# Routing one-hots of a Mamba-plus-MoE block: place one-hots built without values on VectorE, top-2 taken from the logits, instruction order laid out anew

## The reference

```python
router_logits = x_flat @ gate_w                      # 2048 tokens x 8 experts
router_probs = jax.nn.softmax(router_logits, axis=-1)
topk_w, topk_idx = jax.lax.top_k(router_probs, TOP_K)          # TOP_K = 2
topk_w = topk_w / jnp.sum(topk_w, axis=-1, keepdims=True)
...
h = jax.nn.silu(ragged_dot(x_rep_sort, w1, group_sizes)) * ragged_dot(x_rep_sort, w3, group_sizes)
out_sort = ragged_dot(h, w2, group_sizes)            # M = 896
...
out = jnp.einsum('tkd,tk->td', out_rep, topk_w)
return x + out
```

## Time and profile before

| | us |
|---|---|
| median of 3 runs | 792.99 |
| range of the runs | 791.93 to 797.85 |
| the profiled execution, whole | 797.66 |
| its span, first to last instruction | 795.8 |
| PE busy in the span | 736.1 (93%) |
| DVE busy | 600.4 (75%) |
| POOL busy | 305.4 (38%) |
| ACT busy | 242.0 (30%) |
| mean granted PE clock | 0.954 |

### The profile page before, as it was taken

One profiled execution on the slowest core, in us unless ns is written; L12 is line 12 of the kernel. 1 busy time (PEld: TensorE's weight loads), 2 busy tenths in 40 slices (PEclk: granted clock), 3 DMA queues, 4 the chain that ended last, 5 costly groups with the idle time before them and its releaser, 6 DMA issues.

```text
span 795.8 us, 10296 instructions
## 1 busy us (share of the span) xinstructions
PE 736.1 (93%) x2771; PEld 476.5 (60%) x2772; DVE 600.4 (75%) x1486; ACT 242.0 (30%) x485; POOL 305.4 (38%) x506
## 2 busy tenths in 40 slices
PE   6979799999999999996679999999999999999993
PEld 4456565586558668664445666666666666666662
DVE  3899988698965676474436888888888888888880
ACT  1547737455784452311001111111111111111110
POOL 2142523333223622129962333444333444333322
PEclk9979989999999999996659999999999999999997
DMA  9402003000400360501008951121111112111111
GB/s 319 131 1 107 0 1 107 0 1 28 133 1 1 102 228 2 192 0 54 0 14 297 304 165 27 26 31 31 31 26 26 26 26 33 33 26 26 26 14 20
DMA packets 31437, 52.10 MB, mean 65 GB/s; under 512 B 3216, under 2 KB 23120, under 8 KB 31408
## 3 DMA queue, kind: packets, MB, share of 16 engines
q1 hardware_dynamic: 23920, 41.51, 15.1%
q0 software_dynamic: 7488, 10.23, 7.8%
HBM read 42.10 MB, written 9.63 MB: 65 GB/s over the span
## 4 chain that ended last, share of the span: by engine, by line
PE 70%; DVE 11%; POOL 8%; issue 7%; DMA 1%; ACT 1%; DVEq 0%; POOLq 0%
PE ps L1025 28%; PE ps L1038 14%; POOL big L2187 5%; PE ps L731 4%; PE ps L403 3%; PE ps L717 3%; PE ps L705 3%; PE ps L458 3%; DVE big L1544 3%; PE ps L582 2%; PE ps L525 2%; PE ps L472 2%; DVE big L1564 2%; DVE big L2070 2%; PE ps L539 1%
## 5 line engine op out<-in xcount | busy, mean ns | idle before, releaser
L2070 DVE STREAM_TRANSPOSE big<-big 32x224 f32<-32x224 f32 x608 | 244.8, 403 | 9.1
L1025 PE MATMUL ps<-big 128*128 x624 | 241.2, 539 | 1.1 <-ACT big L1450 1.1
L1025 PEld LDWEIGHTS ps<-big 128*128 128x128 f32 x624 | 118.4, 190 | 105.2 <-issue 103.4
L1038 PE MATMUL ps<-big 128*128 x546 | 124.5, 380 | 2.1 <-DVE big L2090 1.3
L2113 POOL TENSOR_TENSOR big<-big 128x1 f32<-128x1 f32 x153 | 48.2, 315 | 202.1 <-DVE big L2078 152.5
L1038 PEld LDWEIGHTS ps<-big 128*128 128x128 f32 x546 | 100.8, 190 | 15.0 <-issue 2.9
L1456 ACT ACTIVATE big<-ps 128x896 f32<-128x896 f32 x39 | 35.8, 917 | 215.6 <-PE ps L1025 215.6
L2085 DVE TENSOR_TENSOR big<-big,ps 128x896 f32<-128x896 f32 x39 | 42.4, 1088 | 48.3 <-PE ps L1025 48.2
L2336 POOL DMA_INDIRECT out_rows<-big x39 | 62.9, 1612 | 22.7 <-issue 22.7
L403 PEld LDWEIGHTS ps<-big 128*128 128x128 f32 x325 | 41.2, 145 | 46.6 <-issue 28.1
L403 PE MATMUL ps<-big 128*128 128x128 f32 x325 | 54.0, 281 | 14.0 <-DVE big L1645 3.5
(11 more groups left out here) (183 smaller groups left out, 967.5 us busy)
## 6 DMA issues: line engine op xcount, KB each, us to landing
big<-in_w SPq DMA_DIRECT2D x24, 896.0 KB, 7.6
big<-cum_rows SPq DMA_DIRECT2D x16, 512.0 KB, 5.3
out_rows<-big SPq DMA_DIRECT2D x4, 512.0 KB, 2.9
xn_rows<-big SPq DMA_DIRECT2D x4, 512.0 KB, 3.1
big<-in_hidden SPq DMA_DIRECT2D x1, 1536.0 KB, 12.1
big<-in_in_proj SPq DMA_DIRECT2D x1, 1288.0 KB, 7.1
big<-in_gate SPq DMA_DIRECT2D x1, 640.0 KB, 13.2
big<-in_up SPq DMA_DIRECT2D x1, 640.0 KB, 8.7
```

Source lines behind the costliest of these rows:

```text
L1025: last = mm(bank(bk + n)[:, 0:HALF], xT[:, k, :], expert_cols(e, off + k * M + n * HALF, HALF), start=(k == 0), stop=(k == KD - 1))
L1038: last = mm(bank(7)[:, 0:D], hTs[:, half, j * P:(j + 1) * P], expert_cols(e, 2 * KD * M + j * D, D), start=(j == 0), stop=(j == MB - 1))
L2070: last = V.transpose(hTs[c * SQ:(c + 1) * SQ, half, :].rearrange("p (j t) -> p j t", j=MB)[:, :, q * SQ:(q + 1) * SQ], ha[q * SQ:(q + 1) * ...
```

## The change

Per engine, what differs:

- **POOL**: the 64 `slots` instructions go.
- **DVE**: `slots(n)` is now one `is_equal` over 8 x 128 elements per sequence (4 x 128 per half), with no value in it. The values go to the list side: `route_block` multiplies token numbers and weights into the block one-hot, and `route_list(n, i)` writes one list for tokens and one for weights, 8 x 128 elements each (before: 4 x 128 each, one per choice). `route_hot` becomes `route_place` (3 instructions) and `route_block` (4).
- **Routing arithmetic on DVE**: top-2 is taken from the logits, with no softmax ahead; exp is taken of one difference per token and feeds only the weights (`route_weigh`, `route_rec`). `route_max` is gone; per part of the work 26 DVE instructions from the maximum to the slots where there were 33 (whole sequence).
- **PE**: `place_` makes for each chunk and choice two products of N = 128 instead of one of N = 256, after one product over zeros that opens the bank. `mlp_down(3, 3)` moves ahead of `turn_half(0)`. `WARM_ROWS` is 4.
- **Order**: the lists of all engines are written anew, in the first stage too; the last part of DVE's is below. `slots`, `route_place` and the lists of sequences 0 and 1 stand between the `hidden_(3, j)`, those of sequence 2 around the last `add_mlp`.

```diff
-WARM_START, WARM_LAST, WARM_ROWS = 5, 8, 5
+WARM_START, WARM_LAST, WARM_ROWS = 5, 8, 4
...
-                pe.wait_ge(hot_placed, nth(n, CH, t))
-                pe.wait_ge(hot_ready, TOP * (n + 1 if n < SEQS - 1 or t < CH // 2 else n + 2))
+                part = n if t < HALVES[0][1].stop or n < SEQS - 1 else SEQS
+                pe.wait_ge(hot_placed, part + 1)
+                pe.wait_ge(hot_ready, 2 * (part + 1))
                 if n == 0 and t == 0:
                     pe.wait_ge(off_scaled, SEQS * (CH - 1))
+
+                    mm(bank(STATES)[:, 0:2 * P], ident[0:P - REST, :], hid[0:P - REST, JB - 1, 0:2 * P], start=True, stop=False)
                 for k in range(TOP):
-                    last = mm(bank(STATES)[:, 0:2 * P], hot_list[n][:, t, k, :], hot_slot[n][:, t, k, :],
-                              start=(n + t + k == 0), stop=(n == SEQS - 1 and t == CH - 1 and k == TOP - 1))
+                    for i, hot in enumerate((hot_token, hot_weight)):
+                        last = mm(bank(STATES)[:, i * P:(i + 1) * P], hot[n][:, t * TOP + k, :], hot_slot[n][:, t * TOP + k, :],
+                                  start=False, stop=(n == SEQS - 1 and t == CH - 1 and k == TOP - 1 and i == 1))
...
             mlp_down(3, 0)
             mlp_down(3, 1)
             mlp_down(3, 2)
+            mlp_down(3, 3)
             turn_half(0)
-            mlp_down(3, 3)
             half_logits(0)
...
+            def route_pick(n, ts=ALL, seq=None):
+                seq = n if seq is None else seq
+                top_.start(n)
+                v.wait_ge(lg_taken, n + 1)
+                top_.then(V.tensor_reduce(rmx[:, ts], lg[:, ts, :], AX, ALU.max))
...
+            def route_next(n, ts=ALL, seq=None):
+                seq = n if seq is None else seq
+                o1, o2 = (picked[seq][:, ts, k, :] for k in range(TOP))
+                top_.then(V.scalar_tensor_tensor(rq[:, ts, :], o1, LEAST, lg[:, ts, :], ALU.mult, ALU.add))
+                top_.then(V.tensor_reduce(rmx2[:, ts], rq[:, ts, :], AX, ALU.max))
+                pick(rq, rmx2, o2, rm2, ts)
+                top_.end()
+                if 0 < n < SEQS:
+                    v.wait_ge(pos_ps, n)
+                V.tensor_tensor(sel[:, ts, :], o1, o2, ALU.add).then_inc(sel_ready, 1)
+
...
+            def route_weigh(n, ts=ALL):
+                v.wait_ge(sel_ready, n + 1)
+                if 0 < n < SEQS:
+                    v.wait_ge(route_e, n)
+                V.tensor_tensor(rd[:, ts], rmx2[:, ts], rmx[:, ts], ALU.subtract).then_inc(route_d, 1)
...
                 v.wait_ge(route_e, n + 1)
...
+                weigh_.start(n)
+                weigh_.then(V.tensor_scalar(rden[:, ts], re_[:, ts], 1.0, None, ALU.add))
+                weigh_.then(V.reciprocal(weight[seq][:, ts, 0], rden[:, ts]))
...
+                steps.then(V.tensor_tensor(picked_pos[:, ts, :, :], picked[seq][:, ts, :, :],
+                                           rpos[:, ts, :].unsqueeze(2).to_broadcast([P, ts.stop - ts.start, TOP, E]), ALU.mult))
+                steps.then(V.tensor_reduce(slotf[seq][:, ts, :], picked_pos[:, ts, :, :], AX, ALU.add))
...
+            def route_place(n, ts=ALL, seq=None):
...
                 v.wait_ge(ssy_ready, SEQS * CH)
                 hot_.start(n)
...
+                hot_.then(V.tensor_tensor(upto_q[:, q, :], entries(slotf[seq], ts).unsqueeze(2).to_broadcast([P, m, LIST + 1]), firsts, ALU.is_ge))
                 hot_.then(V.tensor_reduce(q1[:, q], upto_q[:, q, :], AX, ALU.add))
...
+            def route_block(n, ts=ALL, seq=None):
...
+                V.tensor_tensor(is_q[:, q, :], upto_q[:, q, 0:LIST], upto_q[:, q, 1:LIST + 1], ALU.subtract)
+                v.wait_ge(place_ready, n + 1)
+                hot_.then(V.tensor_tensor(token[:, ts, :], cst[:, at_ + ts.start:at_ + ts.stop].unsqueeze(2).to_broadcast([P, m // TOP, TOP]),
                                           place[seq][:, ts, :], ALU.subtract))
...
+                V.tensor_tensor(token_q[:, q, :], is_q[:, q, :], entries(token, ts).unsqueeze(2).to_broadcast([P, m, LIST]), ALU.mult)
...
+                hot_.then(V.tensor_tensor(weight_q[:, q, :], is_q[:, q, :], entries(weight[seq], ts).unsqueeze(2).to_broadcast([P, m, LIST]), ALU.mult))
...
+            def route_list(n, i, ts=ALL, seq=None):
                 seq = n if seq is None else seq
...
+                v.wait_ge(hot_step, 4 * (n + 1))
+                V.tensor_tensor((hot_token, hot_weight)[i][seq][:, q, :].rearrange("p k (e i) -> p k e i", e=E),
+                                picked[seq][:, ts, :, :].rearrange("p t k e -> p (t k) e").unsqueeze(3).to_broadcast([P, m, E, LIST]),
+                                (token_q, weight_q)[i][:, q, :].unsqueeze(2).to_broadcast([P, m, E, LIST]),
+                                ALU.mult).then_inc(hot_ready, 1)
...
+            def slots(n, ts=ALL, seq=None):
...
-                V.tensor_tensor(hot_list[seq][:, ts, k, :].rearrange("p t (e i) -> p t e i", e=E),
-                                picked[seq][k][:, ts, :].unsqueeze(3).to_broadcast([P, m, E, LIST]),
-                                is_q[seq][:, q, :].rearrange("p (t k) i -> p t k i", k=TOP)[:, :, k, :].unsqueeze(2).to_broadcast([P, m, E, LIST]),
-                                ALU.mult).then_inc(hot_ready, 1)
+                V.tensor_tensor(hot_slot[seq][:, q, :], cst[:, C_SLOT:C_SLOT + P].unsqueeze(1).to_broadcast([P, m, P]),
+                                entries(place[seq], ts).unsqueeze(2).to_broadcast([P, m, P]), ALU.is_equal).then_inc(hot_placed, 1)
...
             scores(0, 3)
             apart(1, 0, 0)
+            apart(1, 0, 1)
             state(0, 2)
-            apart(1, 0, 1)
-            h1_(0, 0)
 
             y_(0, 2)
+            masked_G(1)
+            apart(1, 1, 0)
+            ln1_h(2)
             off(0, 3)
-            masked_G(1)
-            ln1_h(2)
-            apart(1, 1, 0)
+            h1_(0, 1)
             apart(1, 1, 1)
-            scores(1, 0)
-            h1_(0, 1)
-            hT1(2)
 
...
+            route_weigh(1)
+            route_slots(1)
+            route_place(1)
+            slots(0)
+            hidden_(3, 0)
+            slots(1)
+            hidden_(3, 1)
+            route_list(0, 0, ALL, None)
+            route_list(0, 1, ALL, None)
             route_rec(1)
-            route_slots(1)
-            hidden_(3, 0)
-            hidden_(3, 1)
-            route_max(2, ALL, 0)
+            route_block(1)
...
             ln2_stats(3, HALVES[1][1], 4, 1)
-            route_max(3, HALVES[0][1], 3, half_rt)
             xn_(4, HALVES[1][1], 3)
-            route_hot(2)
-            route_pick(3, HALVES[0][1], 3, half_rt)
-            route_next(3, HALVES[0][1], 3, half_rt)
-            route_rec(3, HALVES[0][1], 3, half_rt)
             route_list(2, 0, ALL, None)
             route_list(2, 1, ALL, None)
+            route_pick(3, HALVES[0][1], 3)
+            route_next(3, HALVES[0][1], 3)
+            route_weigh(3, HALVES[0][1])
+            route_pick(4, HALVES[1][1], 3)
+            route_next(4, HALVES[1][1], 3)
+            route_weigh(4, HALVES[1][1])
+            route_rec(3, HALVES[0][1], 3)
+            route_rec(4, HALVES[1][1], 3)
             route_slots(3, HALVES[0][1], 3, half_rt)
-            route_max(4, HALVES[1][1], 3, half_rt)
-            route_pick(4, HALVES[1][1], 3, half_rt)
-            route_next(4, HALVES[1][1], 3, half_rt)
-            route_hot(3, HALVES[0][1], 3)
-            route_rec(4, HALVES[1][1], 3, half_rt)
+            route_place(3, HALVES[0][1], 3)
+            route_block(3, HALVES[0][1], 3)
             route_list(3, 0, HALVES[0][1], 3)
+            slots(3, HALVES[0][1], 3)
+            route_slots(4, HALVES[1][1], 3, half_rt)
             route_list(3, 1, HALVES[0][1], 3)
-            route_slots(4, HALVES[1][1], 3, half_rt)
-            route_hot(4, HALVES[1][1], 3)
+            route_place(4, HALVES[1][1], 3)
+            slots(4, HALVES[1][1], 3)
+            route_block(4, HALVES[1][1], 3)
             route_list(4, 0, HALVES[1][1], 3)
             route_list(4, 1, HALVES[1][1], 3)
             table()
...
-            def slots(n, t, seq):
...
-                    for i in range(2):
-                        last = G.tensor_scalar(hot_slot[seq][:, t, k, i * P:(i + 1) * P], cst[:, C_SLOT:C_SLOT + P],
-                                               place[seq][:, t, k:k + 1], rec[seq][:, t, k, i:i + 1], ALU.is_equal, ALU.mult)
-                last.then_inc(hot_placed, 1)
```

More of the change, by code:

```diff
@@ L37 @@
 SERIES = 8
+LEAST = -3.0e38
 F32 = mybir.dt.float32
@@ L1894, in _ @@
             masked_G(2)
+            h1_(1, 1)
+            hidden_(0, 2)
+            apart(2, 2, 1)
+            apart(2, 3, 0)
+            apart(2, 3, 1)
+            scores(2, 0)
+            hidden_(0, 3)
+            ln1_h(3)
+            off(1, 3)
+            hT1(3)
             hidden_(0, 4)
-            ln1_h(3)
-            scores(2, 0)
```

(53 more changed lines are left out.)

666 lines of the change are left out of this document (311 added, 355 removed).

## The result

The changed kernel takes 773.1 us (median of 4 runs, 771.48 to 775.11) beside 795.4 for the kernel before on the same chip: a ratio of 0.972 (0.967 to 0.978). It is faster by 22 us. The forecast was 763, and its range of 754 to 773 ends just under the median.

A forecast was written before the change was run, and what follows sets the result against it. POOL's 64 one-hots were taken to bound the routing stage up to `choose`. Gains of 26.7 (routing), 0.3 (after `choose`) and 3.0 (first stage) sum to 30.0 us: 792.99 to 763.0, range 754 to 773.

The forecast's parts named there:

- The routing chain: MLP's end to `choose`: with POOL's 53.1 us removed, DVE's ten-step chain sets the length; `choose` at 384.1, 26.7 us gained.
- 64 + 64 products of two passes each: PE's 16 `place_` calls in routing, N = 128: 0.86 us a call as before, 13.8 us for all.
- The low clock: Rival, routing: PE low from 357 on becomes the bound, `choose` 9 us later, 772 us; chance 0.11.
- over 90% was to be the sign: Sign of being right: DVE busy over 90% from the MLP's end to `choose`, with the table last.
- DVE's work between the `hidden_(3, j)`: Last sequence's MLP: 12.6 us of DVE work added, some 28 of 30 busy; costed at nothing, else 1 to 4 us.
- `out_(0, 2)`: First stage, PE's 2.92 us wait for `h1_(0, 1)`: comes 2 us earlier, wait under 1 us.
- I take 3 us gained: First stage's new order: 3 us gained, a third for PE's low clock; bounds 14 gained and 6 lost.
- gives nothing or loses up to 6: Rival, first stage: the new order gains nothing or loses up to 6 us, total 766 to 772; chance 0.16.
- the last MLP later than 324 us: Sign of being wrong, end of first stage: PE reaches the last sequence's MLP later than 324 us.
- The product less: After `choose`: one warm product less in L739 saves 0.9 us, of which the gather leaves about 0.3.
- From `choose` on nothing changes: After `choose`: nothing changes but one warm product less; L739 is 4.61 us for 10 passes.

The follow-up runs named there:

- The experiment on the kernel before: The kernel before with one POOL call, `ln2_scale(4)`, moved ahead of all 64 place one-hots: 797.55 us in one execution, `choose` at 411.19.
- warm9: The changed kernel with 18 idle products instead of 8 before the first transpose of gathered rows: 771.84 us (771.29 to 776.03).

## Why the forecast was right and wrong

**The routing chain: right, step by step.** The forecast's ten steps, with the difference of the starts in DVE's rows above, from the MLP's end at 362.20 (the first ends with L1808 at 364.77) to `choose` at 387.79:

| step | forecast | measured |
|---|---|---|
| 1 last `add_mlp`, `slots(2)`, variance | 2.4 | 2.6 |
| 2 POOL's root and hop | 0.8 | 0.8 |
| 3 `xn_(4)` | 0.8 | 0.7 |
| 4 two lists of 1024 | 2.4 | 2.3 |
| 5 top-2, half 3 | 2.7 | 2.9 |
| 6 top-2, half 4 | 2.8 | 2.6 |
| 7 weights | 1.5 | 1.2 |
| 8 half 3's place, block, list | 4.2 | 4.0 |
| 9 half 4's | 5.4 | 4.9 |
| 10 table | 4.1 | 3.7 |
| sum | 27.1 | 25.6 |

The step that was bounded from the furthest rows, an operation of 1024 elements, came at 1.21 us, like `scores`, and the doubly repeated inputs cost nothing. POOL's root took 0.70, near the 0.72 with DVE idle beside it. `table()` did end last, as forecast: its one-hot (L1791) at 387.68, 0.1 us before `choose`, while ACT's copy of the lists, which the profile names as the releaser of `choose`, had ended at 386.87. PE took 3.67 us for four `place_` calls at the full clock (365.10 to 368.77), where the forecast had 3.5; its "64 + 64 products of two passes each" is twice what its sum uses, the profile has 128 rows for all 16 calls. The low clock came only with the last four, and cost nothing since the table still ended later. DVE is busy 85% from the MLP's end to `choose`, where over 90% was to be the sign. The experiment on the kernel before bears out that POOL's amount of work was the limit.

**DVE's work between the `hidden_(3, j)`: right in that it cost nothing.** From 329.87 to 362.20 DVE is busy 24.7 of 32.3 us, less than the forecast's 28 of 30, and PE all of it.

**`out_(0, 2)`: right and worth nothing.** The wait fell from 2.92 to 0.51 us as forecast, and 7 us further on `dt_(2)` waits 2.80. DVE is the limit there (60.7 of 63 us busy, before 61.1): PE was let go earlier and met the next thing that DVE hadn't done.

**The first stage: the step that failed.** "I take 3 us gained" was taken from the one wait that could be seen to go, with nothing for what comes in its place. Measured is a loss of 5.4 us in the first pair of profiles and 7.0 between the means, beside 5.4 us between medians on one chip (771.5 and 766.1). That is the forecast's own rival "gives nothing or loses up to 6" at its far end, which alone would have given 772; and the forecast's own sign of being wrong, the last MLP later than 324 us, is in the profile (329.87). Its argument stood in the text (3.4 us of idle time to win in the long part, a full DVE at 40 to 103), and was outweighed by one row. A gain could only come from idle time, and there DVE set the pace; a loss could come anywhere. The runs show waits in place of the one that went: 12.6 us of idle time from 40 to 160 us where the old order has 8.0, and 4.1 where it has 0.7 from 160 to 280. PE's low clock isn't the difference: summed over the stretches to 160 us (share missing times busy time), it costs 8.8 us on average in the new order's six profiles and 9.2 in the old one's five, from 6.7 to 12 in single ones.

**After `choose`: mis-sized.** The product less was to gain 0.3. `choose` to the first rows did get shorter by 0.9 us, but not by the product less: `warm9`, with 18 idle products, needs the same 5.1 us. PE ran at the full clock, so the gather was issued 2.04 us after `choose` began (before 2.51), and the rows no longer waited for L739. The idle products were done in 1.97 us where L739 took 4.61, so PE stood idle for 2 us, and the first tile's products took 7.97 instead of 6.32 us. "From `choose` on nothing changes" took the 4.61 us as a price of ten products; it was the price at the low clock, which the waits for POOL had caused and the change removed.

**The number.** 30.0 us were to be gained; 28.4 - 5.4 - 0.5 = 22.5 were, by the profiles, and 22.3 by the medians. That is 7.7 of the 10.1 us between 763.0 and 773.1. The other 2.4 are the base: the kernel before had a median of 792.99 in three runs and of 795.42 in the four beside the changed kernel. With the old order and the longer stretch of idle products the same routing change brings 796.6 to 765.4, 31 us.

## What to carry over

When a stage was paced by one engine, count the next chain instruction by instruction from the point that starts it: durations from the trace gave 27.1 for a measured 25.6 us. Don't credit a rewritten order with a wait that it removes unless the engine that ended the wait has room for it: where that engine is full, the wait comes back at the next instruction that needs it, and where PE has next to no idle time a new order has nothing to win and can only add waits. And when you shorten a stage, look at what clock its filler ran: filler that was long enough at the low clock may leave a gap at the full one. What such a gap costs isn't the same in every execution.
